# An attention and mixture-of-experts kernel: index columns named earlier in VectorE's step, weight pieces split by one line over all tiles

## The chip, the cores and the metric

One core of one Trainium2 chip runs the whole program. The metric is the device time of one execution in microseconds (us); for the kernel before, the median of three timed executions is given, and one further execution was profiled.

## What is computed

The reference is one transformer layer on 16 sequences of 56 tokens (896 tokens, width 512), all in float32:

```python
x = x + xattn(layernorm(x), ctx_4096, Wq, bq, Wk, bk)   # one head over 1500 context rows of 512 per sequence
x = x + ffn(layernorm(x), gate_w, bias, Wg, Wu, Wd, Sg, Su, Sd)

# ffn, with E = 16 experts of inner width 256, and 4 experts for each token:
scores = sigmoid(x @ gate_w.T) + bias
topk_w, topk_idx = top_k(scores, 4)
topk_w = topk_w / (sum(topk_w) + 1e-20)
z   = silu(x @ Wg[e].T) * (x @ Wu[e].T) * weight_of(token, e)
out = sum_e z @ Wd[e].T + silu(x @ Sg.T) * (x @ Su.T) @ Sd.T
```

Which tokens go to which expert is known only on the chip. With the inputs of the reference the 16 experts get 55, 484, 523, 0, 0, 470, 0, 0, 0, 6, 398, 338, 82, 102, 790 and 336 tokens (worked out from the reference alone).

## The kernel before

**Two stages.** The first stage (to about 280 us) streams the context through TensorE for eight pairs of sequences. The second stage is the feed-forward part: seven tiles of 128 tokens through the shared expert, and then the routed tiles. The change touches the second stage alone.

**Tiles and turns.** The tokens of an expert are cut into tiles of up to 128 rows. An expert with at least one token is a *turn*. The counts above give 11 turns of 1, 4, 5, 4, 1, 4, 3, 1, 1, 7 and 3 tiles, 34 tiles in all. I number these tiles u = 0 to 33; the code's own `t` is u + 7, because `SHARED` is 7 (the shared expert's tiles come first). The tables of the loop (which turn, which expert, which column of the list of rows, how many weight pieces must be asked for) are made on VectorE in `find_turns` and `fill_tables`, and go by way of TensorE (`lay_tables`) into one row of integers, `plan`. Each engine reads an entry of it into a register with `entry` (L323), which the trace shows as a `TENSOR_LOAD` on that engine's sequencer.

**Weights.** An expert's weights (1.5 MB) come by DMA into `w_raw`, one of three sets. They are split into a high and a low part, in three pieces (`THIRDS`) for each turn, 33 pieces in all: ScalarE makes `w_hi` (L896), VectorE then makes `w_lo` = `w_raw` - `w_hi` (L1279). `more_thirds(t)` on either engine makes as many pieces as the plan's entry T_PIECES for tile t asks for beyond those made; SyncE loads the set of a later turn as soon as the pieces that free it are done (the wait is on `lo_ready`). TensorE waits in `split_turn` before the first tile of a turn.

**One step of the loop.** Every engine runs its own list for tile t:

- TensorE: transpose of z(t-1) (L702), low part of the up product of t (L679 on `taken_lo`), transpose of tile t+1 (L499), down product of t-1 (L679 on `zt_hi`, then on `zt_lo`), high part of the up product of t+1 (L679 on `taken_hi`, `w_hi` and `w_lo`).
- ScalarE: `zt_hi`(t-1) (L917), `half_tanh`(t) (L912), `taken_hi`(t+1) (L907), `y_sb`(t-2) (L925, which waits until the add that last read this half of `y_sb`, that of t-4, has landed), the row numbers for the add of t-2, `add_at` (L930), and then its pieces `w_hi`.
- VectorE: `zt_lo`(t-1) (L1314), `gated_rows` and `z_rows` of t (L1335, L1323), `taken_lo`(t+1) (L1298), the routing weights `taken_w` of t+1 (`take_weight`, L1309), the row numbers for the gather of t+3, `take_at` (`name_take`, L1305), and then its pieces `w_lo`.
- GpSimd, in strict order: the gather of tile t+5 (`gather`, L444, an indirect DMA, which needs `take_at` of t+5), then the add of tile t into the output in HBM (`add`, L459, an indirect DMA that accumulates, which needs `y_sb` and `add_at` of t). The first tile of a turn also waits until every earlier add has landed, because another expert may hold the same tokens.

Of the kernel before, what the change touches and what calls it, by code (L numbers as in the profile page):

```python
# [8 lines left out]
EXPERTS, INNER, TOPK = 16, 256, 4  # L9
P = 128  # L10
# [21 lines left out]
SETS = 3  # L32
THIRDS = 3
# [4 lines left out]
SHARED = TOKENS // P  # L38
# [34 lines left out]
def moe_attention_kernel(nc, x, ctx, ctx_t, wq, bq, wk, bk, gate_t, gate_b, experts, shared,  # L73
# [14 lines left out]
    with es:  # L88
        def sb(name, shape, dt=fp32):
            return es.enter_context(nc.sbuf_tensor(name, shape, dt))  # L90
# [111 lines left out]
        upto = sb("upto", [P, 1])  # L202
# [17 lines left out]
        expert_t = sb("expert_t", [P, 1])  # L220
        col_t = sb("col_t", [P, 1])
        turn_t = sb("turn_t", [P, 1])
        size_t = sb("size_t", [P, 1])
        done_t = sb("done_t", [P, 1])
        share_t = sb("share_t", [P, THIRDS])
        ready_t = sb("ready_t", [P, THIRDS])
        thirds_t = sb("thirds_t", [P, 1])
        all_thirds = sb("all_thirds", [P, 1])
        all_turns = sb("all_turns", [P, 1])
        last_turn = sb("last_turn", [P, 1])  # L230
# [62 lines left out]
        def settle(eng):  # L293
            eng.sem_inc(waited, 1)
# [26 lines left out]
        def entry(eng, table, at, most):  # L321

            return eng.value_load(plan[0:1, bass.ds(at + table, 1)], min_val=0, max_val=most)  # L323
# [86 lines left out]
        def _(pool):  # L410
# [29 lines left out]
            def gather(t, i):  # L440

                pool.wait_ge(take_named, t - (SHARED - 1))
                settle(pool)
                nc.gpsimd.indirect_dma_start(  # L444
                    taken[i][:, :], None, h_rows[:, :], bass.IndirectOffsetOnAxis(ap=take_at[i][:, 0:1], axis=0)
                    ).then_inc(gathered[i], 16)
# [565 lines left out]
        def _(dve):  # L1012
# [237 lines left out]
            def fill_tables():  # L1250

                ch.link(nc.vector.tensor_tensor(is_turn_e[:], is_turn_e[:], iota16, ALU.mult))
                ch.mark(nc.vector.scalar_tensor_tensor(col_t[:], expert_t[:], float(TILES_MAX), upto[:], ALU.mult, ALU.add))
                ch.mark(nc.vector.tensor_tensor(size_t[:], end_t[:], first_t[:], ALU.subtract))
                ch.mark(nc.vector.tensor_tensor(done_t[:], upto[:], first_t[:], ALU.subtract))
                ch.mark(nc.vector.tensor_scalar_add(last_turn[:], all_turns[:], -1.0))
                ch.mark(nc.vector.tensor_scalar(all_thirds[:], all_turns[:], float(THIRDS), None, ALU.mult))
                ch.mark(nc.vector.tensor_tensor(is_first[:], first_t[:], upto[:], ALU.is_equal))
                ch.link(nc.vector.tensor_scalar(halves[:], half_at[:], tiles_upto[:, EXPERTS - 1:EXPERTS], None, ALU.is_lt))

                ch.mark(nc.vector.tensor_scalar(share_t[:], iota16[:, 1:1 + THIRDS], size_t[:], 1.0 / THIRDS, ALU.mult, ALU.mult))
                ch.mark(nc.vector.tensor_scalar_add(done_t[:], done_t[:], 1.25))
                ch.mark(nc.vector.tensor_tensor(tables[:, 1:2], col_t[:], first_t[:], ALU.subtract))
                ch.mark(nc.vector.tensor_scalar_min(tables[:, 2:3], expert_t[:], float(EXPERTS - 1)))
                ch.mark(nc.vector.tensor_tensor(tables[:, 4:5], turn_t[:], last_turn[:], ALU.min))
                ch.mark(nc.vector.scalar_tensor_tensor(tables[:, 5:6], first_t[:], float(SHARED), is_first[:], ALU.add, ALU.mult))
                ch.mark(nc.vector.reduce_sum(tables[:, 6:7], is_turn_e[:], axis=AX.X))
                ch.mark(nc.vector.reduce_sum(tables[:, 7:8], halves[:], axis=AX.X))
                ch.link(nc.vector.tensor_copy(tables[:, 0:1], all_turns[:]))
                ch.link(nc.vector.tensor_scalar(ready_t[:], share_t[:], done_t[:], None, ALU.is_le))  # L1270
                ch.link(nc.vector.reduce_sum(thirds_t[:], ready_t[:], axis=AX.X))
                ch.link(nc.vector.scalar_tensor_tensor(thirds_t[:], turn_t[:], float(THIRDS), thirds_t[:], ALU.mult, ALU.add))
                ch.link(nc.vector.tensor_scalar_add(thirds_t[:], thirds_t[:], float(THIRDS)))
                ch.mark(nc.vector.tensor_tensor(tables[:, 3:4], thirds_t[:], all_thirds[:], ALU.min))
                dve.wait_ge(dve_step, ch.now())
                dve.sem_inc(tables_ready, 1)

# [27 lines left out]
                nc.vector.tensor_copy(take_at[i][:], list_at[:, bass.ds(col, 1)]).then_inc(take_named, 1)  # L1305

            def take_weight(t, i):
                e = entry(dve, T_EXPERT, t - SHARED, EXPERTS - 1)
                nc.vector.tensor_copy(taken_w[:, i:i + 1], taken[i][:, bass.ds(e + DIM, 1)]).then_inc(w_ready, 1)  # L1309

# [72 lines left out]
            dve.wait_ge(hi_ready, THIRDS)  # L1383
            third_lo(2 * THIRD)
            n_inner = inner_pairs(dve)
            taken_to_lo(SHARED)
            take_weight(SHARED, 1)
            name_take(SHARED + 2, 1)

            def step(t, i):  # L1390
                z_to_lo(t - 1)
                silu_rows(t, i)
                taken_to_lo(t + 1)
                take_weight(t + 1, 1 - i)
                name_take(t + 3, 1 - i)
                more_thirds(t + 1)

            more_thirds(SHARED)
# [72 lines left out]
```

## Time and profile before

| | us |
|---|---|
| median of three executions | 553.05 |
| the three | 546.88, 553.05, 556.69 |
| the profiled execution, its own time | 548.86 |
| its span, first to last instruction | 547.1 |
| stretch of the routed loop on TensorE (first up product of tile 0 to that of tile 33) | 321.2 to 521.7 |

| engine | busy us | share of the span |
|---|---|---|
| TensorE, matmul | 490.3 | 90% |
| TensorE, weight load | 293.8 | 54% |
| VectorE | 259.4 | 47% |
| ScalarE | 155.4 | 28% |
| GpSimd | 110.8 | 20% |

### The profile page before, as it was taken

Reading aid. Unit: us, or ns where it says so; the run is one execution under the profiler, and the core shown is the slowest. Engines: PE = TensorE matmul, PEld = TensorE weight load, DVE = VectorE, ACT = ScalarE, POOL = GpSimd, SP = SyncE. Lnnn points to the kernel's source line nnn. Section 1 sums busy time; section 2 is a strip of 40 time slices with the busy share of each in tenths; the row PEclk is TensorE's granted clock in tenths of the full one; section 3 lists DMA queues with packets and bytes.
Section 4 is the critical chain, followed back from the end, with each engine's and each line's share of the span. In section 5 each row is a group of like instructions: output and inputs, shape, how many; then the busy total and the mean of one; then the engine's idle time right before and its main releaser. Section 6 shows DMA issues by size and latency. Waiting matters only on the chain.

```text
span 547.1 us, 10804 instructions
## 1 busy us (share of the span) xinstructions
PE 490.3 (90%) x2472; PEld 293.8 (54%) x2473; DVE 259.4 (47%) x707; ACT 155.4 (28%) x303; POOL 110.8 (20%) x100
## 2 busy tenths in 40 slices
PE   3999999999999999999899878989898988899970
PEld 1583535353636363543467646767676656577740
DVE  3203337373645445453448874545455646545420
ACT  0000402020203021210222263435363545444430
POOL 1000000000000000000002233444344442444431
PEclk9969999999999999999799989999898999899985
DMA  9999999999999999999646667876749585455552
GB/s 214 399 423 424 388 424 419 411 428 401 427 400 425 400 423 411 417 426 418 241 114 159 157 207 197 270 230 115 195 124 261 98 212 174 80 84 108 97 64 32
DMA packets 28231, 149.04 MB, mean 272 GB/s; under 512 B 4072, under 2 KB 4200, under 8 KB 16424
## 3 DMA queue, kind: packets, MB, share of 16 engines
q1 hardware_dynamic: 15832, 123.08, 56.6%
q0 software_dynamic: 8720, 20.21, 20.2%
q10 hardware_dynamic: 3664, 5.57, 3.3%
q8 instruction: 7, 0.11, 0.1%
q14 instruction: 8, 0.07, 0.0%
HBM read 133.84 MB, written 15.01 MB: 272 GB/s over the span
## 4 chain that ended last, share of the span: by engine, by line
PE 67%; DMA 14%; issue 6%; DVE 4%; ACT 3%; DVEq 2%; ACTq 2%; POOLq 1%; POOL 0%; SPq 0%
PE b L573 16%; PE scores L549 15%; PE b L679 14%; DMA out<-y_sb,add_at 10%; PE b L537 6%; PE b L499 4%; PE scores L679 3%; DMA w_raw<-in_experts 3%; PE scores L511 2%; PE b L563 2%; DMA w_qk<-in_wk 1%; PE b L586 1%; DVEq L323 1%; ACTq L323 1%; ACT w_hi L896 1%
## 5 line engine op out<-in xcount | busy, mean ns | idle before, releaser
L573 PE MATMUL b<-ctx_rows,probs_t 125*64 125x512 f32 (+1 forms) x384 | 86.4, 600 | 0.0
L549 PE MATMUL scores<-ctx_cols,g_t 128*64 128x500 f32 x384 | 84.8, 586 | 0.0
L459 POOL DMA_INDIRECT out<-y_sb,add_at x34 | 54.6, 1605 | 52.2 <-ACT add_at L930 21.8
L423 POOL TENSOR_TENSOR rstd<-var_eps,neg_half 128x1 f32<-128x1 f32 x16 | 8.8, 551 | 268.5 <-DVE var_eps L1021 268.5
L1279 DVE TENSOR_TENSOR w_lo<-w_raw,w_hi (+1 forms) x33 | 39.7, 1223 | 41.2 <-ACT w_hi L896 29.8
L679 PE MATMUL b<-w_hi,taken_hi 128*128 x136 | 57.5, 423 | 1.1 <-ACT taken_hi L907 1.1
L679 PE MATMUL b<-w_lo,taken_hi 128*128 x136 | 55.9, 411 | 0.0
L573 PEld LDWEIGHTS b<-ctx_rows,probs_t 125*64 125x64 f32 (+1 forms) x384 | 26.4, 138 | 48.3 <-issue 47.4
L549 PEld LDWEIGHTS scores<-ctx_cols,g_t 128*64 128x64 f32 x384 | 26.3, 137 | 48.3 <-issue 48.3
L444 POOL DMA_INDIRECT taken<-h_rows,take_at x34 | 34.1, 1002 | 76.4 <-DVE take_at L1305 74.7
L896 ACT CAST w_hi<-w_raw (+1 forms) x33 | 33.8, 1048 | 31.3 <-issue 15.1
L679 PE MATMUL b<-w_hi,taken_lo 128*128 x136 | 40.0, 416 | 0.0
L1052 DVE TENSOR_REDUCE row_max<-scores 128x1 f32<-128x1500 f32 x8 | 13.8, 1721 | 47.2 <-PE scores L549 47.2
L835 ACT COPY h_t_now<-b 128x512 f32<-128x512 f32 x7 | 4.1, 586 | 109.4 <-PE b L499 109.4
L537 PE MATMUL b<-xn_t,w_fold 128*128 128x128 f32 x256 | 33.1, 291 | 1.4 <-ACT xn_t L819 1.4
L679 PEld LDWEIGHTS b<-w_hi,taken_hi 128*128 128x128 f32 x136 | 27.3, 200 | 13.0 <-issue 7.1
L537 PEld LDWEIGHTS b<-xn_t,w_fold 128*128 128x128 f32 x256 | 31.7, 205 | 2.1 <-issue 1.1
L917 ACT CAST zt_hi<-b 128x256 fp32r<-128x256 f32 x41 | 15.2, 371 | 54.7 <-PE b L702 54.6
L1314 DVE TENSOR_TENSOR zt_lo<-b,zt_hi 128x256 fp32r<-128x256 f32 x41 | 17.2, 421 | 28.2 <-ACT zt_hi L917 26.0
L679 PEld LDWEIGHTS b<-w_lo,taken_hi 128*128 128x128 f32 x136 | 27.2, 200 | 5.6
L907 ACT CAST taken_hi<-b 128x512 fp32r<-128x512 f32 x41 | 24.1, 587 | 16.4 <-PE b L499 14.9
L1298 DVE TENSOR_TENSOR taken_lo<-b,taken_hi 128x512 fp32r<-128x512 f32 x41 | 28.1, 684 | 1.4 <-ACT taken_hi L907 1.3
(213 smaller groups left out, 682.0 us busy)
## 6 DMA issues: line engine op xcount, KB each, us to landing
ctx_rows<-in_ctx SPq DMA_DIRECT2D x48, 1024.0 KB, 15.0
ctx_cols<-in_ctx_t SPq DMA_DIRECT2D x32, 1500.0 KB, 17.8
w_raw<-in_experts SPq DMA_DIRECT2D x11, 1536.0 KB
h_rows<-h ACTq DMA_DIRECT2D x16, 115.5 KB
taken<-h_rows SPq DMA_DIRECT2D x7, 264.0 KB
out<-xs ACTq DMA_DIRECT2D x2, 784.0 KB
shared_raw<-in_shared SPq DMA_DIRECT2D x1, 1536.0 KB, 32.3
xs<-in_x ACTq DMA_DIRECT2D x12, 112.0 KB
```

Source lines behind the costliest of these rows:

```text
L444: nc.gpsimd.indirect_dma_start(taken[i][:, :], None, h_rows[:, :], bass.IndirectOffsetOnAxis(ap=take_at[i][:, 0:1], axis=0)).then_inc(gath ...
L459: nc.gpsimd.indirect_dma_start(out[:, :], bass.IndirectOffsetOnAxis(ap=add_at[i][:, 0:1], axis=0), y_sb[:, i * DIM:(i + 1) * DIM], None, c ...
L499: last = nc.tensor.transpose(bank[:, k * P:(k + 1) * P], src[:, k * P:(k + 1) * P], ident)
L537: last = nc.tensor.matmul(b7[:, m * P:(m + 1) * P], w_fold[:, k, m * P:(m + 1) * P], xn_t[:, k, :], start=(k == 0), stop=(k == KD - 1))
L549: last = nc.tensor.matmul(scores[HALF * b:HALF * (b + 1), n, 0:CHUNK], g_t[:, k, HALF * b:HALF * (b + 1)], ctx_cols[:, at:at + CHUNK], sta ...
L573: last = nc.tensor.matmul(b3[HALF * b:HALF * (b + 1), :], probs_t[0:rows_in(p), at:at + HALF], ctx_rows[0:rows_in(p), g, b, c * DIM:(c + 1 ...
L679: return nc.tensor.matmul(bank, a[:, k, :], w[:, bass.ds(at + k * n, n)], start=start, stop=stop)
L896: nc.scalar.copy(w_hi[:, bass.ds(at, THIRD)], w_raw[:, bass.ds(at, THIRD)]).then_inc(hi_ready, 1)
L907: nc.scalar.copy(taken_hi[:].rearrange("p k n -> p (k n)"), b4[:, :]).then_inc(taken_hi_ready, 1)
L1279: nc.vector.tensor_tensor(w_lo[:, bass.ds(at, THIRD)], w_raw[:, bass.ds(at, THIRD)], w_hi[:, bass.ds(at, THIRD)], ALU.subtract).then_inc(l ...
L1298: nc.vector.tensor_tensor(taken_lo[:].rearrange("p k n -> p (k n)"), b4[:, :], taken_hi[:].rearrange("p k n -> p (k n)"), ALU.subtract).th ...
L1314: nc.vector.tensor_tensor(zt_lo_cols[:], b5[:, 0:INNER], zt_hi_cols[:], ALU.subtract).then_inc(zt_lo_ready, 1)
```

## The change

It has two parts and some waits.

1. In VectorE's `step`, `take_weight(t + 1, ...)` and `name_take(t + 3, ...)` move from behind `taken_to_lo(t + 1)` to the head of the step, ahead of `z_to_lo(t - 1)`; ahead of the loop, `taken_to_lo(SHARED)` moves behind them. So within VectorE's list they stand behind the weight pieces of the step before instead of ahead of those of the same step. `take_weight` now waits for the gather of its tile to land and for `z_rows`; `gather` on GpSimd now also waits for the transposes of the tile that last held its buffer (`tt_ready`).
2. In `fill_tables`, the number of weight pieces that must have been asked for by a tile no longer follows that tile's place within its own turn, but one straight line over all tiles, (u + 1) / tiles x 3 x turns + 4. It is bounded below by what the next tile needs and above by what the three sets of weights can hold.

```diff
@@ gather
                 pool.wait_ge(take_named, t - (SHARED - 1))
                 settle(pool)
+                pool.wait_ge(tt_ready, t - 1)
+                settle(pool)
@@ fill_tables
-                ch.mark(nc.vector.tensor_tensor(size_t[:], end_t[:], first_t[:], ALU.subtract))
-                ch.mark(nc.vector.tensor_tensor(done_t[:], upto[:], first_t[:], ALU.subtract))
+                ch.mark(nc.vector.tensor_scalar(is_last[:], end_t[:], -1.0, upto[:], ALU.add, ALU.is_equal))
+                ch.mark(nc.vector.reciprocal(per_tile[:], tiles_upto[:, EXPERTS - 1:EXPERTS]))
...
+                ch.mark(nc.vector.tensor_scalar_add(line_t[:], upto[:], 1.0))
...
-                ch.mark(nc.vector.tensor_scalar(share_t[:], iota16[:, 1:1 + THIRDS], size_t[:], 1.0 / THIRDS, ALU.mult, ALU.mult))
-                ch.mark(nc.vector.tensor_scalar_add(done_t[:], done_t[:], 1.25))
+                ch.mark(nc.vector.scalar_tensor_tensor(line_t[:], line_t[:], per_tile[:], all_thirds[:], ALU.mult, ALU.mult))
+                ch.mark(nc.vector.tensor_tensor(need_t[:], turn_t[:], is_last[:], ALU.add))
+                ch.mark(nc.vector.tensor_tensor(most_t[:], turn_t[:], is_first[:], ALU.subtract))
...
-                ch.link(nc.vector.tensor_scalar(ready_t[:], share_t[:], done_t[:], None, ALU.is_le))
-                ch.link(nc.vector.reduce_sum(thirds_t[:], ready_t[:], axis=AX.X))
-                ch.link(nc.vector.scalar_tensor_tensor(thirds_t[:], turn_t[:], float(THIRDS), thirds_t[:], ALU.mult, ALU.add))
-                ch.link(nc.vector.tensor_scalar_add(thirds_t[:], thirds_t[:], float(THIRDS)))
-                ch.mark(nc.vector.tensor_tensor(tables[:, 3:4], thirds_t[:], all_thirds[:], ALU.min))
+                ch.mark(nc.vector.tensor_scalar(need_t[:], need_t[:], float(THIRDS), float(THIRDS), ALU.mult, ALU.add))
+                ch.link(nc.vector.tensor_scalar(most_t[:], most_t[:], float(THIRDS), float(SETS * THIRDS), ALU.mult, ALU.add))
+                ch.link(nc.vector.scalar_tensor_tensor(line_t[:], line_t[:], float(THIRDS + 1), most_t[:], ALU.add, ALU.min))
+                ch.link(nc.vector.tensor_tensor(line_t[:], line_t[:], need_t[:], ALU.max))
+                ch.mark(nc.vector.tensor_tensor(tables[:, 3:4], line_t[:], all_thirds[:], ALU.min))
@@ take_weight
             def take_weight(t, i):
+                dve.wait_ge(gathered[i], (t - SHARED) // 2 * 16 + 16)
+                settle(dve)
+                dve.wait_ge(z_rows_ready, t - 1)
+                settle(dve)
@@ ahead of the loop, and the step
-            taken_to_lo(SHARED)
             take_weight(SHARED, 1)
             name_take(SHARED + 2, 1)
+            taken_to_lo(SHARED)

             def step(t, i):
+                take_weight(t + 1, 1 - i)
+                name_take(t + 3, 1 - i)
                 z_to_lo(t - 1)
                 silu_rows(t, i)
                 taken_to_lo(t + 1)
-                take_weight(t + 1, 1 - i)
-                name_take(t + 3, 1 - i)
                 more_thirds(t + 1)
```

## Rows read from the trace of the kernel before

**Rows 1.** The page: engines' busy time, and TensorE's granted clock in 40 slices.
```profile
PE 490.3 (90%) x2472; PEld 293.8 (54%) x2473; DVE 259.4 (47%) x707; ACT 155.4 (28%) x303; POOL 110.8 (20%) x100
PEclk9969999999999999999799989999898999899985
```
**Rows 2.** Waits, 290 to 547 us: engine, line, releaser, total, times, longest.
```profile
POOL taken L444 <- DVE take_at L1305: 74.7, 30, 6.6
...
DVE w_lo L1279 <- ACT w_hi L896: 29.8, 15, 4.2
...
ACT y_sb L925 <- DMA out<-y_sb,add_at: 22.1, 10, 4.7
```
**Rows 3.** Waits of TensorE's matmuls from 320 us on.
```profile
PE b L679 <- ACT zt_hi L917: 7.0, 4, 2.5
PE scores L679 <- ACT zt_hi L917: 4.2, 2, 2.4
PE b L679 <- DVE zt_lo L1314: 3.0, 3, 1.5
```
**Rows 4.** Timeline of TensorE: start, us; two tiles' transposes, nothing waited for between.
```profile
481.43 0.63 PE L499 MATMUL b<-cst,taken 128*128 128x128 f32 x4
...
486.79 0.63 PE L499 MATMUL b<-cst,taken 128*128 128x128 f32 x4
```
**Rows 5.** Timeline of GpSimd around tile 4's add; idle time in brackets.
```profile
362.28 1.58 POOL L459 DMA_INDIRECT out<-y_sb,add_at  x1 [1.13 <-DMA out<-y_sb,add_at]
367.88 0.98 POOL L444 DMA_INDIRECT taken<-h_rows,take_at  x1 [4.02 <-DVE take_at L1305]
369.81 1.58 POOL L459 DMA_INDIRECT out<-y_sb,add_at  x1 [0.94 <-issue]
```
**Rows 6.** Timeline of ScalarE in the step of u = 5.
```profile
356.76 0.59 ACT L907 CAST taken_hi<-b 128x512 fp32r<-128x512 f32 x1 [0.48 <-PE b L499]
358.69 0.59 ACT L925 COPY y_sb<-b 128x512 f32<-128x512 f32 x1 [1.34 <-DMA out<-y_sb,add_at]
359.40 0.19 ACT L930 COPY add_at<-list_to 128x1 int32 x1
361.28 1.05 ACT L896 CAST w_hi<-w_raw  x1 [1.69 <-issue]
362.24 0.37 ACT L917 CAST zt_hi<-b 128x256 fp32r<-128x256 f32 x1
363.24 0.61 ACT L925 COPY y_sb<-scores 128x512 f32<-128x512 f32 x1
```
**Rows 7.** Timeline of TensorE: the late down products of u = 5, 10 and 13.
```profile
363.13 0.49 PE L679 MATMUL b<-w_hi,zt_hi 128*128 x1 [1.34 <-ACT zt_hi L917]
...
393.01 0.69 PE L679 MATMUL scores<-w_hi,zt_hi 128*128 x1 [2.39 <-ACT zt_hi L917]
...
413.63 1.19 PE L679 MATMUL b<-w_hi,zt_lo 128*128 x2 [1.53 <-DVE zt_lo L1314]
```
**Rows 8.** Granted clock in stretches of 10 us (PE, PEld, DVE, ACT, POOL; PEclk, DMA, GB/s).
```profile
390.00:400.00 10.00, 7.61 (x31) 5.99 (x32) 4.95 (x10) 4.88 (x11) 3.33 (x4) 0.83 0.40 79
...
480.00:490.00 10.00, 9.91 (x47) 7.24 (x46) 5.56 (x14) 5.10 (x11) 4.49 (x4) 1.00 0.45 87
```
**Rows 9.** Timeline of VectorE in the step of u = 3, one piece in it.
```profile
346.83 0.68 DVE L1298 TENSOR_TENSOR taken_lo<-b,taken_hi 128x512 fp32r<-128x512 f32 x1
347.50 0.15 DVE L1309 COPY taken_w<-taken 128x1 f32 x1
348.33 0.15 DVE L1305 COPY take_at<-list_at 128x1 int32 x1 [0.68 <-issue]
350.13 1.22 DVE L1279 TENSOR_TENSOR w_lo<-w_raw,w_hi  x1 [1.64 <-issue]
351.27 0.42 DVE L1314 TENSOR_TENSOR zt_lo<-b,zt_hi 128x256 fp32r<-128x256 f32 x1
```
**Rows 10.** The line of table reads: count and ns min/median/max, on VectorE.
```profile
L323 DVEq TENSOR_LOAD <-plan x99: 298/306/986, 329.0 to 522.8; - x99
```

More of the change, by code:

```diff
@@ L222, in moe_attention_kernel @@
         turn_t = sb("turn_t", [P, 1])
[L223 to L227, printed above, removed]
+        is_last = sb("is_last", [P, 1])
+        per_tile = sb("per_tile", [P, 1])
+        line_t = sb("line_t", [P, 1])
+        need_t = sb("need_t", [P, 1])
+        most_t = sb("most_t", [P, 1])
         all_thirds = sb("all_thirds", [P, 1])
```

## Prediction

> **What bounds the kernel now.** I read the page first. TensorE is busy 90% of the span, and nothing else comes near [rows 1]; the time is TensorE's work plus the gaps in it and the stretches at the lower clock. The first 280 us are not touched, so I asked the waits and the timeline only from there on.
>
> The floor of the routed loop: between two tiles' transposes lie 5.36 us with no wait [rows 4]; eight such stretches lie between 5.32 and 5.54, and I take 5.34 as the floor. Tile 0's up product starts at 321.2 and tile 33's at 521.7: 200.5 us for 33 tiles, where the floor gives 176.2. So 24.3 us of the loop are losses, and only these can move.
>
> What the losses are: TensorE waits 11.2 us for `zt_hi` in six places and 3.0 us for `zt_lo` in three [rows 3] (2.1 of the 11.2 in the last tile, behind the loop). After three of these waits the granted clock falls. The slice from 390 to 400 us has 0.83 [rows 8], which is 3.4 us at 1.2 GHz instead of 2.4, and half of that, 1.7 us, is lost; the slices from 410 and from 470 read the same. A fourth, from 320, lies at the start of the loop.
>
> Why `zt_hi` is late: in the step of u = 5 ScalarE holds back `y_sb` until 358.69, because the add that last read its buffer hasn't landed, and so `w_hi` comes at 361.28 and `zt_hi` behind it at 362.24 [rows 6]. TensorE had stood 1.34 us for it [rows 7]. ScalarE waits for an add's landing ten times, 22.1 us [rows 2]. And why does the add land late? GpSimd stands in order: the add of tile 4 starts at 369.81, though its `y_sb` began at 363.24 [rows 5, 6]. Between them stands the gather of tile 9, which waited 4.02 us for `take_at` and started at 367.88. That wait is GpSimd's largest, 74.7 us in 30 waits [rows 2]. So the chain is: `take_at` late, gather late, add late, `y_sb` late, piece late, `zt_hi` late, TensorE idle, at times a slower clock.
>
> **The change, part by part.**
>
> *A, `take_at` earlier.* `name_take` moves up nearly one tile. What holds the gather of tile 9 next is its new wait, the transposes of tile 7. These end near 361.8 (TensorE's timeline has them from 361.16, 0.63 us long). With GpSimd's usual 0.9 us from the semaphore [rows 5] the gather goes at about 362.8, 5 us sooner. The add of tile 4 then waits for `add_at`, which ends 0.7 us and a copy behind the start of `y_sb` (358.69, then 359.40 [rows 6]), and goes at about 364.9 instead of 369.8. A buffer of `y_sb` is asked for again two tiles, 10.7 us, after it was filled; an add's landing takes 5 to 8.5 us in the chain of waits, so start plus landing is now 6.7 to 10.2 us after `y_sb`. Nearly all the ten waits go; the ten turn starts, whose adds wait for the landing before, keep a remainder. Of TensorE's waits the three at u = 5, 10 and 19 hang on this alone: 1.34 and 2.39 [rows 7] and 2.48, in sum 6.2 us, with one fall of the clock (390 to 400), 1.7 us. But `zt_lo` is needed 1 us after `zt_hi`, and it comes out of VectorE: by the times below, u = 5 gets back 1.0 and u = 19 2.1 of their waits. I take 5.8 + 1.7 = **7.5 us gained**.
>
> *B, pieces on a line.* Worked out from the turns' sizes, the plan asked for pieces in 21 steps; three at once before the tiles u = 14, 22 and 23, whose turns have one tile each or follow such a one. The line asks in 23 steps: at most one a step until u = 13 and none in that step, two at once before u = 15, two before u = 22, and still three before u = 23. The burst at u = 13 cost the 1.53 us of [rows 7], 0.54 before it, and the clock's 1.7 at 410 to 420: 3.8. Against this a pair costs: `w_lo` takes 1.22 [rows 9] and `w_hi` 1.05 [rows 6], so one piece more in a step delays `zt_lo` by about 1.2, and with the copies behind it 1.5. The burst before u = 22 shrinks by one piece, but part 1 of the change puts the copies behind it: 0.3 gained. The one before u = 23 stays. Sum: 3.8 - 1.5 + 0.3 = **2.6 us gained**. SyncE's queue: the sets are freed earlier, so every load is issued no later than before, and each landed before its first piece. One exception is the third set, on which the piece of u = 1 waits now as before. The two instructions that `fill_tables` gains, at about 0.16 us, are under 0.4 us and stand beside the shared tiles; the links of the chain become one fewer. I put them at nothing.
>
 Before, this ran while VectorE would anyway have waited for ScalarE's `w_hi`: `w_lo` waited 29.8 us for it in 15 steps [rows 2]. That cover is gone in steps with a piece. From the start of `w_lo` to `zt_lo` it was 1.14 us [rows 9]; now the sequencer can run on while `w_lo` computes, and needs 0.2 + 0.4 + 1.66 + 0.2 = 2.5. So in a step where `w_hi` decides, `zt_lo` would be 1.3 later. In a step where `w_hi` is early, `w_lo` starts up to 1.66 sooner, and `zt_lo` comes no later or 0.3 sooner. With the add's wait gone `w_hi` ends 3.37 us after `taken_hi`(t+1) starts, which is about 1.95 us after the up product that follows. That puts `zt_lo` at 4.6 us behind that up product where 4.3 is wanted, and the lateness halves itself, since a late TensorE starts the next `taken_hi` late: 0.17 a step. Table reads that take 0.6 to 1.0 instead of 0.306 [rows 10] now lie behind the wait instead of under it; about one in six does, which is 0.1 a step more. So 22 steps with one piece x 0.25 = 5.5 us. The two first steps with pieces, which wait for the weights' DMA, cost 0.75 and 1.3. Sum: **7.5 us lost**. Bounds for C: nothing (if every `w_hi` is early), and 1.3 a step, 22 x 1.3 + 2 = 31 us (if none is and no slack takes it). I stand near the low end, because before the change VectorE's sequencer was as full and single-piece steps took 5.44 to 5.54 us, hardly more than the floor.
>
> A rule weighed: for a table read the row has 0.306 us at the median [rows 10]. The Trainium skill (DMA: Bandwidth & Descriptors, Latency and other measured facts) states a floor of about 0.6 us for a tensor load, which this trace contradicts in most of its 99 reads. By that figure C would be 22 x 0.6 = 13 us dearer, and the change would lose about 11.
>
> *New waits.* `take_weight` waits for the gather of t+1 with `zt_lo`, `z_rows` and `taken_lo` queued behind it, so TensorE's down product would wait for it too. That gather is now issued two tiles before; the old one went at 367.88 [rows 5] and TensorE, which never waited for a gather [rows 3], read its tile 5.9 us later. I put the wait at nothing, and at most 0.5 us at each of ten turn starts, 5 us.
>
> **Sum:** -7.5 - 2.6 + 7.5 = -2.6 us against the profiled execution's 548.86: 546.3. The tail behind tile 33 (adds that wait for each other) moves along unchanged. The three timed runs have their median at 553.05, 4.2 above the profiled one; in proportion I get 550.5. The slower runs should hold more late landings, which A removes, so I take 549.5.
>
> **The rivals.**
>
> *1, faster: the add chain was all.* If VectorE keeps up (C at nothing), the losses of rows 3 in the loop (9.1 + 3.0) and three falls of the clock (5.1) go, but for the burst before u = 23 (about 4): 13 to 14 us, 2.5%, so 539. For it: VectorE is busy 47% only [rows 1]. Against: its time is its sequencer's, which that share leaves out. Chance 0.13.
>
> *2, slower: VectorE's sequencer becomes the bound.* The place is the stretch from `w_lo` to `zt_lo`. The gains are 10.1, so it decides against the change from (10.1 - 2) / 22 = 0.37 us a step, and makes it slower by 2% from 0.87. At 0.9 a step: 20 + 2 - 10.1 = +12, 565. For it: 15 waits for `w_hi` [rows 2]; against it, the feedback above. By the Trainium skill's figure for a table read (the page and section named above) it would come out this way. Chance 0.1.
>
> *3, the gather's wait at the head of the step stalls.* +5 on top of my sum: 554.5. Chance 0.12.
>
> *4, hidden anyway.* GpSimd's adds stay late since the new wait on the transposes or the landings hold them; nothing moves but B and C: 553.05 - 2.6 + 7.5, at most 558, at least 551. Chance 0.1.
>
> **How the numbers follow.** My forecast has 0.55; with rivals 3 and 4 that gives 0.77 within 2% (about what a measurement of this kernel can tell from no change, 11 us), faster 0.13, slower 0.1. The range reaches from just above rival 1 to the far end of rival 4: 540 to 557.5. Its own spread for the forecast is 544 to 555.
>
> **What would show it.** A right: GpSimd's wait for `take_at` falls from 74.7 to under 20 us, replaced by one for the transposes; adds start 3 to 5 us sooner; `y_sb`'s wait for landings falls from 22.1 to under 6; the slice from 390 is at full clock. B right: `w_lo` comes three at a time once in the loop, and no fall of the clock stands near tile 14. C right: `w_lo` to `zt_lo` grows from 1.14 to about 2.5 us and TensorE's waits for `zt_lo` grow from 3.0 to 6 to 10 us in many small ones. I am wrong if TensorE's waits for `zt_lo` stay near 3 us (rival 1) or exceed 15 (rival 2), or if `taken_w` waits for gathers (rival 3).

## The result, and the profile after

| | before | after |
|---|---|---|
| median of 18 executions, us | 554.22 | 559.29 |
| the same, lowest to highest | 546.88 to 560.58 | 556.53 to 562.20 |
| the profiled execution, its own time | 548.86 | 556.53 |
| its span | 547.1 | 554.7 |
| routed loop on TensorE, first up product of tile 0 to that of tile 33 | 200.5 | 208.2 |

The ratio is 1.0126 (95% interval 1.0096 to 1.0156): slower by 1.3%, where I had forecast 549.5 us and at most 557.5. It leaves out executions more than 1.5% above the fastest of their kernel, seven of the kernel before and none of the changed one, and so lies above the quotient of the two medians (1.009). The profiled executions differ by 7.7 us and their loops by 7.7 us as well: all of it is in the loop.

The waits of the changed kernel from 290 us to its end (engine, line, releaser, total, times, longest), beside [rows 2, 3]:

```profile
POOL taken L446 <- DVE take_at L1309: 53.4, 17, 6.4
DVE w_lo L1283 <- ACT w_hi L898: 40.5, 25, 5.0
ACT w_hi L898 <- PE b L681: 15.6, 12, 3.4
ACT w_hi L898 <- PE scores L681: 13.5, 9, 1.8
PE scores L681 <- DVE zt_lo L1322: 12.5, 12, 2.1
ACT y_sb L927 <- DMA out<-y_sb,add_at: 7.1, 4, 4.5
PE b L681 <- DVE zt_lo L1322: 5.7, 9, 1.3
PE b L681 <- ACT zt_hi L919: 4.2, 2, 2.2
```

`y_sb` waits 7.1 us for landings where it waited 22.1: that gain came. But TensorE now waits for `zt_lo` 21 times, 18.2 us, where it was 3.4 in four (the 3.0 of [rows 3], and 0.4 for a product into `scores` that I had left out). Two rows that I had no eye for have grown: ScalarE's `w_hi` waits 29.1 us in 21 steps for TensorE's *down product* (the semaphore that `more_thirds` waits for is counted up by nothing else). In the kernel before these rows were

```profile
ACT w_hi L896 <- PE scores L679: 5.4, 4, 2.5
ACT w_hi L896 <- PE b L679: 5.1, 4, 1.6
```

Two tiles of the changed kernel, on three engines (start and duration in us, idle time in brackets). VectorE:

```profile
365.98 1.23 DVE L1283 TENSOR_TENSOR w_lo<-w_raw,w_hi  x1 [1.17 <-ACT w_hi L898]
367.44 0.15 DVE L1317 COPY taken_w<-taken 128x1 f32 x1 [0.24 <-issue]
368.27 0.15 DVE L1309 COPY take_at<-list_at 128x1 int32 x1 [0.68 <-issue]
368.42 0.42 DVE L1322 TENSOR_TENSOR zt_lo<-b,zt_hi 128x256 fp32r<-128x256 f32 x1
...
371.93 1.22 DVE L1283 TENSOR_TENSOR w_lo<-w_raw,w_hi  x1 [1.53 <-ACT w_hi L898]
373.90 0.15 DVE L1317 COPY taken_w<-taken 128x1 f32 x1 [0.74 <-issue]
375.20 0.15 DVE L1309 COPY take_at<-list_at 128x1 int32 x1 [1.15 <-issue]
375.35 0.42 DVE L1322 TENSOR_TENSOR zt_lo<-b,zt_hi 128x256 fp32r<-128x256 f32 x1
```

TensorE's last product of each down product, and ScalarE's piece behind it:

```profile
368.99 0.70 PE L681 MATMUL b<-w_hi,zt_lo 128*128 x2 [0.18 <-DVE zt_lo L1322]
...
375.92 0.70 PE L681 MATMUL scores<-w_hi,zt_lo 128*128 x2 [1.03 <-DVE zt_lo L1322]
```
```profile
364.59 1.05 ACT L898 CAST w_hi<-w_raw  x1 [0.96 <-PE scores L681]
...
370.54 1.05 ACT L898 CAST w_hi<-w_raw  x1 [0.95 <-PE b L681]
```

Read them as a ring. `zt_lo` starts at 368.42; the product on it at 368.99 (+0.57), and it ends at 369.69 (+0.70). `w_hi`, which waits for that end, starts at 370.54 (+0.85), `w_lo` at 371.93 (+1.39), and behind the two reads and copies `zt_lo` at 375.35 (+3.42). That is 6.93 us for one tile; the other half of the loop's body takes 5.61 (from 362.81 to 368.42), since there `w_lo` to `zt_lo` is 2.44. Both are over the floor of 5.34 [rows 4]. Two of the other links hardly vary: in the 21 steps in which `w_hi` waits for a down product, `w_lo` starts 1.38 to 1.39 us behind it, and in 19 of them the product starts 0.57 us behind `zt_lo`; from the product's end to `w_hi` it is 0.5 to 1.0. Before, the last link was 1.14 [rows 9]; with it the same sum gives 4.3 to 4.7 us (an estimate from the links), under the floor, so that the ring never showed.

The pair of tiles thus costs 12.5 us, where two times the floor is 10.7. In the loop TensorE's waits for `zt_lo` grew by 14.8 us, those for `zt_hi` shrank by 5.2, and the small gaps that end with "issue" or at a transpose by about 3. The three falls of the granted clock (from 321.0, 341.5 and 426.9) last 3.4, 6.8 and 3.4 us and cost as much as the four before.

### The profile page after: what moved, and what is told of

It is laid out like the page before. It is cut to its first block, busy times and chain, and to the rows that moved or that the text cites. A ratio compares the mean times of both kernels' runs of the same rounds, so it can differ in the third digit from the quotient of the medians.

```text
span 554.7 us, 10946 instructions
## 1 busy us (share of the span) xinstructions
PE 490.8 (88%) x2472; PEld 291.8 (53%) x2473; DVE 261.7 (47%) x709; ACT 156.8 (28%) x303; POOL 111.6 (20%) x100
## 4 chain that ended last, share of the span: by engine, by line
PE 60%; DMA 12%; issue 8%; DVEq 5%; ACT 4%; DVE 4%; ACTq 3%; POOLq 1%; SPq 0%; POOL 0%
PE b L575 15%; PE scores L551 15%; PE b L681 10%; DMA out<-y_sb,add_at 7%; PE b L539 6%; DMA w_raw<-in_experts 4%; DVEq L323 3%; PE b L501 3%; ACT w_hi L898 3%; PE scores L513 2%; PE scores L681 2%; PE b L565 2%; ACTq L323 2%; DMA w_qk<-in_wk 1%; DVE zt_lo L1322 1%
## 5 line engine op out<-in xcount | busy, mean ns | idle before, releaser
L446 POOL DMA_INDIRECT taken<-h_rows,take_at x34 | 34.2, 1007 | 81.7 <-DVE take_at L1309 53.4
L919 ACT CAST zt_hi<-b 128x256 fp32r<-128x256 f32 x41 | 15.2, 372 | 62.1 <-PE b L704 62.1
L501 PE MATMUL b<-cst,taken 128*128 128x128 f32 x164 | 25.0, 275 | 2.1 <-issue 1.1
```

The costliest lines, as they stand in the source:

```text
L446: nc.gpsimd.indirect_dma_start(taken[i][:, :], None, h_rows[:, :], bass.IndirectOffsetOnAxis(ap=take_at[i][:, 0:1], axis=0)).then_inc(gath ...
L501: last = nc.tensor.transpose(bank[:, k * P:(k + 1) * P], src[:, k * P:(k + 1) * P], ident)
```

## The experiments

In all tables the ratio is that of a kernel's time to that of the kernel before in the same group of runs, with its 95% interval.

### Each part alone

`plan_only` is the kernel before with the diff of `fill_tables` alone; `order_only` is the changed kernel with the old `fill_tables`.

> The kernel before with the line of pieces alone (fill_tables of the change, nothing else). Theory L (loop): the loss of the changed kernel is a closed ring: w_lo, then the two table reads and copies, then zt_lo, the down product, its yt_ready, the next w_hi, the next w_lo. With the copies in their old place that ring is 0.56 + 0.70 + 0.5 to 0.9 + 1.05 + 0.34 + 1.14 = 4.3 to 4.7 us, under the 5.34 us that TensorE needs for a tile, so the line alone costs nothing and gives what part B of the prediction had, 2.6 us, bounds 0 to 5: ratio 0.991 to 1.000. Theory P (plan): asking for a piece in step after step is what makes the tiles slow; then this kernel alone carries most of the loss, ratio 1.008 to 1.013.

> The changed kernel with the old plan of pieces: only the order on VectorE and the new waits. Theory L: the ring is 5.6 us in one of the two halves of the loop's body and 6.2 to 6.9 in the other in each step with a piece, and pieces stand in 21 steps here; about 0.85 us x 18 = 15 lost, 7 won by the earlier adds, and the bursts of three (2 more lost each with the copies behind them): ratio 1.012 to 1.022, TensorE's waits for zt_lo from 12 us up. Theory P: ratio 0.995 to 1.003.

| | ratio | interval |
|---|---|---|
| plan_only | 1.0117 | 1.0071 to 1.0164 |
| order_only | 1.0225 | 1.0176 to 1.0274 |
| both (the change) | 1.0126 | 1.0096 to 1.0156 |

The effects don't add up: the line costs 1.2% in the old order and gives back 1.0% in the new one. The waits of `plan_only` from 320 us on say a part of why it costs:

```profile
ACT y_sb L925 <- DMA out<-y_sb,add_at: 29.1, 13, 4.7
...
PE scores L679 <- ACT zt_hi L917: 8.0, 4, 3.1
PE b L679 <- ACT zt_hi L917: 7.0, 4, 3.3
PE b L499 <- DMA taken<-h_rows,take_at: 6.1, 3, 4.2
```

The line puts a piece in nearly every step, and in the old order `y_sb` is late in about every third (29.1 us in 13 waits), with the piece and `zt_hi` queued behind it: 15.0 us of waits for `zt_hi` instead of 11.2. The late add was the chain that I had read, and the line meets it more often. That explains only a part of the loss. Of the 7.8 us between the two profiled executions the loop has 3.9; the others lie ahead of it, where TensorE waits 4.2 us for the gather of tile 0. The kernel before and the changed one have no such wait, but `order_only` (3.4) and `early_read_line` (3.8) do, so that it isn't shown to come from the line.

And `order_only` has the new wait at full size:

```profile
PE b L681 <- DVE zt_lo L1320: 13.7, 13, 1.7
PE scores L681 <- DVE zt_lo L1320: 8.6, 8, 2.0
```

### Is it the gather's wait, or the number of reads behind `w_lo`?

`weight_head` has `take_weight` with its two waits at the head and `name_take` in its old place, old plan. `weight_spare1` is that and, at the head, one more read of an index column and its copy into a tile that nobody uses. `spare1` is the kernel before with only such a spare read and copy at the head:

```diff
             def step(t, i):
+                read_spare(t + 1, 1 - i, 1)    # entry(T_COL), copy of list_at into a spare column
                 z_to_lo(t - 1)
```

> The changed order and waits by half, with the old plan: take_weight with its waits for the gather and for z_rows at the head of VectorE's step, name_take where it was. Theory L: one read and copy less in the ring, 0.83 us, and less often a long table read: 4.8 us in one half of the body and 5.4 to 5.9 in the other. So 0.1 to 0.3 a step, 2 to 6 us, and nothing won on the adds: ratio 1.003 to 1.010. Theory G (the wait for the gather at the head of the step costs): the whole loss stays, and grows since the gathers are late again: ratio 1.015 or more. In its trace w_lo to zt_lo is 1.6 to 2.4 us.

> take_weight at the head as in weight_head, and behind it one more table read with a copy into a spare tile that nobody reads; name_take stays in its old place. Nothing is left out of the result. Theory L: the number of reads between w_lo and zt_lo sets the time, whatever they are for: two again, so the ring is 5.6 to 6.9 us as in order_only and the loss is back, without the earlier adds: ratio 1.018 to 1.030, w_lo to zt_lo 2.4 us and up. Theory E (the loss of order_only comes from the gathers and adds going earlier or from the wait for tt_ready): ratio as weight_head, 0.997 to 1.003.

> The kernel before with one table read and one copy of an index column into a spare tile at the head of VectorE's step, ahead of z_to_lo; everything else stays, the two old copies behind taken_to_lo too. The ring theory (zt_lo, down product, w_hi, w_lo, zt_lo) goes by what stands between w_lo and zt_lo: one read and copy of about 0.83 us makes the stretch 2.0 instead of 1.14 us and the ring 5.1 to 5.6 us, hardly over the floor of 5.34, as with take_weight alone at the head (0.9993): ratio 0.998 to 1.010, w_lo to zt_lo 1.9 to 2.3 us. The theory that VectorE's whole list is the bound (three copies now in a step of about 5.9 us, where the kernel before has two) expects 0.8 us more in each step with a piece, 22 x 0.5 or more: 1.02 or more.

| | at the head | reads in a step | ratio | interval |
|---|---|---|---|---|
| weight_head | 1 | 2 | 0.9993 | 0.9964 to 1.0022 |
| order_only | 2 | 2 | 1.0225 | 1.0176 to 1.0274 |
| weight_spare1 | 2 | 3 | 1.0371 | 1.0285 to 1.0456 |
| spare1 | 1 | 3 | 1.0156 | 1.0105 to 1.0207 |

`weight_head` has the wait for the gather and loses nothing, so that wait isn't the cause. One read behind `w_lo` is free, the second costs 2.3%: that is a threshold, as a ring that passes the floor has one. `weight_spare1` cost more than I expected (at most 1.030), and `spare1`, where I had expected at most 1.010, says why. Its VectorE, with no piece in the step:

```profile
522.46 0.42 DVE L1320 TENSOR_TENSOR zt_lo<-b,zt_hi 128x256 fp32r<-128x256 f32 x1
...
523.76 0.68 DVE L1299 TENSOR_TENSOR taken_lo<-b,taken_hi 128x512 fp32r<-128x512 f32 x1
524.56 0.15 DVE L1315 COPY taken_w<-taken 128x1 f32 x1
525.40 0.15 DVE L1306 COPY take_at<-list_at 128x1 int32 x1 [0.68 <-issue]
527.86 0.15 DVE L1311 COPY spare<-list_at 128x1 int32 x1 [2.31 <-issue]
528.01 0.42 DVE L1320 TENSOR_TENSOR zt_lo<-b,zt_hi 128x256 fp32r<-128x256 f32 x1
```

From `zt_lo` to `zt_lo` it is 5.55 us with no wait for another engine: VectorE's own list, mostly its sequencer, is over the floor of 5.34. From `w_lo` to `zt_lo` it is only about 1.5 us in the mean over the steps with one piece, so the ring isn't what holds it. I read from this that there are two bounds near the floor, the ring and the length of VectorE's list, and that a third read hits the second one. This is argued from one trace: a third read was tried only at the head, and in `spare1` TensorE also waits 4.8 us for gathers in four places, which no run separates from the list.

### The same copies elsewhere

`copies_behind` is `order_only`, and `copies_behind_line` the changed kernel, with the copies one instruction later:

```diff
             def step(t, i):
-                take_weight(t + 1, 1 - i)
-                name_take(t + 3, 1 - i)
                 z_to_lo(t - 1)
+                take_weight(t + 1, 1 - i)
+                name_take(t + 3, 1 - i)
                 silu_rows(t, i)
```

> order_only (old plan) with the two copies one place further on: behind z_to_lo(t - 1) and ahead of silu_rows(t), all waits as in the changed kernel. Theory L: no read stands in the ring (4.3 to 4.7 us again), and take_at is still named more than 2 us earlier than before, so the loss of order_only (2.2%) goes; z_rows and taken_lo come some 1.8 us later, which has slack but for a few tenths a step: ratio 0.990 to 1.006. Theory E: the same gathers, adds and waits, so ratio 1.015 to 1.023.

> The changed kernel with the two copies behind z_to_lo(t - 1): line of pieces, early adds, and no read in the ring. Theories L and Y together: both losses gone, ratio 0.980 to 0.998, best of all so far; TensorE's waits for zt_lo under 5 us and ScalarE's for landings under 8. If L is wrong it stays near the changed kernel, 1.010 and more.

| | ratio | interval |
|---|---|---|
| copies_behind | 0.9968 | 0.9930 to 1.0007 |
| copies_behind_line | 1.0009 | 0.9971 to 1.0047 |

With the same waits and the same reads, `order_only`'s ratio is lower by 2.6 points once no read stands between `w_lo` and `zt_lo`. TensorE's waits in `copies_behind` from 320 us on:

```profile
PE b L681 <- ACT zt_hi L919: 7.1, 5, 1.9
PE scores L681 <- ACT zt_hi L919: 4.3, 3, 1.5
PE b L501 <- issue: 3.8, 13, 0.5
PE b L681 <- DVE taken_lo L1300: 1.9, 6, 0.4
PE b L681 <- DVE zt_lo L1320: 1.7, 3, 0.7
```

`zt_lo` costs 1.7 us instead of 22.3. But `taken_lo` now stands behind the reads (6 waits), and the transpose behind it starts late in 13 tiles. The line's version missed its expectation (at most 0.998) by a little; `y_sb` still waited 17.5 us for landings in it, where I had expected under 8. The reads are not free there either; they are cheaper.

### The reads taken out of the stretch, the copies left in

These decide whether the reads' place is the cause. The two table entries are read in the old place, behind `taken_lo` of the step before, into two held registers; the waits and the copies stay at the head, as in the changed kernel.

```diff
+            def read_next(t):
+                dve.reg_mov(next_e, entry(dve, T_EXPERT, t + 1 - SHARED, EXPERTS - 1))
+                dve.reg_mov(next_col, entry(dve, T_COL, t + 3 - SHARED, LISTS + EXPERTS - 1))
...
             def step(t, i):
-                take_weight(t + 1, 1 - i)
-                name_take(t + 3, 1 - i)
+                take_weight(t + 1, 1 - i, dve.snap(next_e, ...))
+                name_take(t + 3, 1 - i, dve.snap(next_col, ...))
                 z_to_lo(t - 1)
                 silu_rows(t, i)
                 taken_to_lo(t + 1)
+                read_next(t + 1)
                 more_thirds(t + 1)
```

> The changed kernel with the old plan of pieces (order_only, 1.0225), but the two table entries of a step are read into held registers in their old place, behind taken_lo of the step before and ahead of more_thirds, and only the four waits and the two copies stand at the head. Same copies at the same place, so take_at is as early; only the reads (0.3 us each and what the sequencer needs to pass the register on) leave the stretch from w_lo to zt_lo. If the reads in that stretch are what costs, w_lo to zt_lo falls from 2.4 to 3.5 us to 1.3 to 1.9, TensorE's waits for zt_lo fall from 22 to under 10 us, and the ratio is 0.990 to 1.005. If the copies and the added semaphore waits cost as much as the reads, or VectorE's list of instructions as a whole is the bound wherever its parts stand, it stays at 1.015 to 1.025.

> The changed kernel itself (1.0126) with the two entries read early in the same way. If only the reads in the stretch cost, the gains that the prediction counted on now show: ratio 0.975 to 0.99, ScalarE's waits for landings about 7 us as in the changed kernel. If the list as a whole is the bound: 1.005 to 1.015.

| | reads at the head | reads behind `taken_lo` |
|---|---|---|
| old plan | 1.0225 (1.0176 to 1.0274) | **0.9895** (0.9862 to 0.9928) |
| the line | 1.0126 (1.0096 to 1.0156) | **0.9861** (0.9826 to 0.9895) |

The place of the reads alone is worth 3.3 points with the old plan and 2.6 with the line (the upper and the lower ratio were taken in different groups of runs, each against the kernel before in its own). `early_read_line` is faster than both kernels: 540.47 us in the median, where the kernel before had 549.17 beside it. Its VectorE in two tiles, which answers to the stretch of the changed kernel above:

```profile
363.27 1.23 DVE L1283 TENSOR_TENSOR w_lo<-w_raw,w_hi  x1 [2.09 <-ACT w_hi L898]
364.41 0.15 DVE L1326 COPY taken_w<-taken 128x1 f32 x1
364.48 0.15 DVE L1317 COPY take_at<-list_at 128x1 int32 x1
364.54 0.42 DVE L1331 TENSOR_TENSOR zt_lo<-b,zt_hi 128x256 fp32r<-128x256 f32 x1
...
368.41 1.23 DVE L1283 TENSOR_TENSOR w_lo<-w_raw,w_hi  x1 [1.90 <-ACT w_hi L898]
369.66 0.15 DVE L1326 COPY taken_w<-taken 128x1 f32 x1
369.80 0.15 DVE L1317 COPY take_at<-list_at 128x1 int32 x1
370.06 0.42 DVE L1331 TENSOR_TENSOR zt_lo<-b,zt_hi 128x256 fp32r<-128x256 f32 x1
```

`w_lo` to `zt_lo` is 1.27 and 1.65 us instead of 2.44 and 3.42, and these two tiles take 10.67 us (`zt_lo` from 364.54 to 375.21) instead of 12.54. The idle time has gone back in front of `w_lo`, where the reads now hide under ScalarE's work. The granted clock and busy shares of its loop (PE, PEld, DVE, ACT, POOL; PEclk, DMA, GB/s) show 86 us at full clock:

```profile
330.00:416.00 86.00, 79.34 (x356) 56.77 (x356) 45.71 (x101) 43.46 (x88) 39.27 (x30) 1.00 0.78 219
```

Its loop takes 189.9 us (323.51 to 513.41), 10.6 less than before.

### The late add, from GpSimd's side

`swap` is the kernel before with the two indirect DMAs of a step exchanged, the add of t ahead of the gather of t+5; `swap_line` adds the line. `behind_line_swap` and `early_read_line_swap` are `copies_behind_line` and `early_read_line` with the same exchange. The two `hi_first` kernels also put ScalarE's `more_thirds` ahead of `keep_y` and `name_add`:

```diff
                 taken_to_hi(t + 1)
+                more_thirds(t + 1)
                 keep_y(t - 2, i)
                 if not isinstance(t, int):
                     name_add(t - 2, i)
-                more_thirds(t + 1)
```

> The kernel before, with the two calls on GpSimd in the loop exchanged: the add of tile t, then the gather of tile t + 5 (and so at the loop's end). VectorE's order is untouched. If late adds are worth what part A of the prediction says (7.5 us and the clock), this gives all of it without the reads in the ring: adds start 3 to 5 us sooner, ScalarE's waits for landings fall from 22 to under 8 us, ratio 0.982 to 0.993. If the adds were not what held TensorE, ratio 0.997 to 1.003.

> swap (add ahead of gather on GpSimd) with the line of pieces. Theory Y: the line alone cost 1.2% because it puts a piece into nearly every step, and ScalarE makes that piece behind the y_sb that waits for an add's landing (29 us in 13 waits in plan_only), so each such wait now reaches zt_hi. With the adds early these waits are gone and the line costs nothing: ratio 0.985 to 0.998, and y_sb waits under 8 us. Theory P (pieces in step after step are slow by themselves): 1.2% above swap, 1.003 to 1.008.

> The changed kernel with its two copies between z_to_lo and silu_rows instead of at the head, and with the add ahead of the gather on GpSimd. No table read stands between w_lo and zt_lo, take_at is early, so the gather behind the add goes as soon as the add has been issued. The two theories together (ring, and late adds holding w_hi and zt_hi back) expect that both kinds of wait go: TensorE's waits for gathers under 5 us (20 in the kernel with the add first and take_at late), ScalarE's waits for landings under 10 us, ratio 0.965 to 0.985. If the landing itself (5 to 8.5 us behind the issue) sets y_sb, the order on GpSimd no longer matters once take_at is early: 0.995 to 1.003, as without the swap (1.0009).

> As the kernel before this in the list, with the add ahead of the gather on GpSimd. take_at is early, so TensorE's waits for gathers should be under 6 us (20 us in 11 where take_at was late), and the late landings of the turn starts shrink too: 0.5 per cent under the kernel before this in the list, 0.97 to 0.985. If the gathers, now 2.5 us later, are waited for by take_weight at the head of VectorE's step, it is 0.99 to 1.01.

> The kernel before with the line of pieces, the add ahead of the gather on GpSimd, and on ScalarE the pieces w_hi ahead of y_sb and add_at. If a late y_sb costs because w_hi stands behind it, the waits of ScalarE for an add's landing no longer reach w_hi and w_lo, and the ratio is 0.965 to 0.985, against 0.985 for the same kernel with y_sb first. If a late y_sb costs because zt_hi of the next step stands behind it, or if the pieces now delay y_sb, add_at and so the adds by 1.05 us, it is 0.985 to 1.005. TensorE's waits for gathers (20 us in 11 in the kernel with y_sb first) should stay.

> As the kernel before this in the list, and on ScalarE the pieces w_hi stand ahead of y_sb and add_at. If late y_sb still held w_hi back there, this gains 0.5 to 1 per cent on it: 0.96 to 0.98. If the pieces ahead of y_sb make add_at and so the adds 1.05 us later, with zt_hi of the next step behind y_sb, it loses as much: 0.98 to 1.00.

| | ratio | interval |
|---|---|---|
| swap | 0.9928 | 0.9893 to 0.9962 |
| swap_line | 0.9849 | 0.9773 to 0.9925 |
| behind_line_swap | 0.9982 | 0.9950 to 1.0014 |
| early_read_line_swap | 0.9957 | 0.9924 to 0.9990 |
| swap_line_hi_first | 1.0560 | 1.0520 to 1.0600 |
| behind_line_swap_hi_first | 1.0573 | 1.0537 to 1.0610 |

`swap` says by another way that the late add cost something, and `swap_line` points to the line costing nothing once adds are early. That is the least certain row: its executions spread from 541.8 to 556.3 us, the ratio rests on four of the ten, and the median of all ten is only 0.4% under that of before. `behind_line_swap` speaks against a large effect: `y_sb` waits 5.6 us for landings in it instead of 17.5, and TensorE 4.3 for gathers, both as I had expected, and yet it is at 0.998 and not at 0.965 to 0.985. What the exchange buys it pays for, in `swap_line`, with late gathers; TensorE from 320 us on, where the kernel before has no such wait:

```profile
PE b L500 <- DMA taken<-h_rows,take_at: 20.5, 11, 5.8
```

With early reads the exchange is a loss of 1% on `early_read_line`, where I had expected a gain of 0.5%. The other case that I had put down came instead: every gather now stands behind a whole add and its waits, and `take_weight` at the head of VectorE's step waits for it, 15.2 us in 8 steps, and TensorE with it:

```profile
DVE taken_w L1327 <- DMA taken<-h_rows,take_at: 15.2, 8, 5.1
PE b L502 <- DMA taken<-h_rows,take_at: 13.0, 9, 3.0
```

`hi_first` was my worst expectation. I had priced the piece ahead of `y_sb` at its 1.05 us. TensorE's waits in `swap_line_hi_first`:

```profile
PE b L500 <- DMA taken<-h_rows,take_at: 40.3, 20, 5.1
```

Its ScalarE shows where that comes from:

```profile
377.09 0.59 ACT L908 CAST taken_hi<-b 128x512 fp32r<-128x512 f32 x1 [1.85 <-PE b L500]
379.59 1.05 ACT L897 CAST w_hi<-w_raw  x1 [1.91 <-PE scores L680]
380.54 0.58 ACT L926 COPY y_sb<-b 128x512 f32<-128x512 f32 x1
```

`w_hi` waits 1.91 us for the down product of t-1, and `y_sb` of t-2, which needs no such thing, now stands behind it; the add follows `y_sb`, and the gather the add. GpSimd's adds wait 77.9 us for `add_at` in 19 places, where it is 28.6 in 11 in `swap_line`, and the granted clock from 320 us to the loop's end is 0.91 in the mean instead of 0.98. It is the same wait for the down product that closes the ring, and I had missed it a second time. This chain is read from the trace; no run takes it apart.

## Why the prediction was wrong, point by point

**The failed step is C's feedback.** It said that `w_hi` ends 3.37 us after `taken_hi`(t+1) starts, and that "the lateness halves itself, since a late TensorE starts the next `taken_hi` late". `taken_hi` isn't what `w_hi` waits for. `more_thirds` on ScalarE waits for `yt_ready`, the down product of the tile before, and that product waits for `zt_lo`. So a late `zt_lo` makes the next `w_hi` late by the whole amount, and nothing is halved; in 21 steps `w_hi` waited for that product. The ring's length replaces the floor as the time of a tile. The right question was not how much later `zt_lo` comes, but whether the ring (0.57 + 0.70 + 0.5 to 0.85 + 1.39 + the stretch from `w_lo`) passes 5.34. With the 2.5 that I had worked out for the stretch it does: 5.66 to 6.0. All of these but the 2.5 stood in the trace of before.

**Its size.** I took 7.5 us for C in all. `early_read_line` is 7.6 us under the kernel before, the changed kernel 7.0 over it, each beside the kernel before in its own group of runs, and between the two stand only the reads. Their place costs 14.6 us, twice the term. That is 0.63 us for each of the 23 steps that ask for pieces (of these 20 ask for one, not the 22 of my sum). A and B together gave those 7.6 us where I had 10.1; so 7.1 of the 9.6 us that the sum is off are C. The mechanism is that of rival 2, which decides against the change from 0.37 a step and makes it slower by 2% from 0.87; it had 0.1. Its stated ground, that VectorE's sequencer time is left out of its 47% [rows 1], was right, its counterargument was the feedback. My sign for it, more than 15 us of waits for `zt_lo`, came: 18.2.

**The argument that VectorE's sequencer "was as full" before** and lost little was wrong: then the reads lay in a stretch where VectorE waited for `w_hi` anyway. The list of instructions kept its length, the ring didn't.

**The slow half of the body.** I added 0.1 us a step for long table reads. In the half that carries the loop's branch, `w_lo` to `zt_lo` is 2.93 to 2.95 us where both reads take their usual 0.3, and in the other half 2.44: the branch is worth 0.5, which I had not counted. The rest of the 3.42 above is a long read, 0.774 us, ahead of `take_at` at 375.20. I had not looked at the two halves apart.

**A was right in the main, and nearly in size.** The slice from 390 is at full clock, as said (1.00 in the windows view, 0.83 in [rows 8]), and waits for landings fall from 22.1 to 7.1 us (I had said under 6). The add of tile 4 starts 2.8 us behind its `y_sb` (371.48 against 368.67) instead of 6.6: 3.8 sooner. With the ring out of the way A is worth 1.05% or 5.8 us (`early_read`, with its copies and waits at the head), against the 7.5 gained that I had forecast. Of the three waits for `zt_hi` that A named, the 1.34 at u = 5 and the 2.39 at u = 10, with the clock's fall behind it, are gone in `early_read`. The third, at u = 19, stays: 2.54 us where it was 2.48, behind a `y_sb` that still waits 3.33 for a landing. All of TensorE's waits for `zt_hi` still sum to 11.3 us there, since others came at the loop's start (1.21 and 2.27). GpSimd's wait for `take_at` fell only to 53.4 in the changed kernel, not under 20, as the head of VectorE's step itself had become late.

**B was treated as independent, and is not.** -2.6 us was forecast. It is +1.2% in the old order, -1.0% in the changed one (though that is a difference of two groups of runs) and -0.3%, within the error, once the reads are early. `w_lo` comes in threes once in the loop, as said. The term that failed is the pair of pieces before tile 15, which I had put at 1.5 us: in `early_read_line` that tile takes 9.9 us (408.9 to 418.8), 4.6 over the floor, with a wait of 3.4 for `zt_hi` and a fall of the clock, where in `early_read` tile 14, with its three pieces, takes 8.0, also with a fall. The changed kernel has its fall at 426.9 in the same tile 15, where I had said that none would stand near tile 14.

**No cost of the new waits shows**: `taken_w` has no wait for a gather in the changed kernel, and `weight_head` is at 0.9993. Rival 3 is out there (its mechanism came in `early_read_line_swap`, with the gathers behind the adds), rival 1 too (18.2 us of waits for `zt_lo`), and rival 4 (waits for landings did fall).

**The rule weighed.** The Trainium skill (DMA: Bandwidth & Descriptors, Latency and other measured facts) puts a tensor load at about 0.6 us at least. The trace of before has 0.306 at the median [rows 10], that of `early_read_line` 0.305 in 106 reads, and the trace decides. That by this figure the change would have lost about 11 us, near the 7 measured, is a coincidence: the dear part was that the reads stood in a ring, not that each was long.

**What stays open.** Taking away ScalarE's wait for the down product, the most direct cut of the ring, wasn't tried, nor `name_take` alone at the head: in both, buffers would have been overwritten while they are still read. The ring is therefore shown by the stretch from `w_lo` to `zt_lo` (lengthened, shortened, reads moved out) and by its other links in the trace, not by a run without that wait. Whether the length of VectorE's list is a bound by itself, why the line alone costs 1.2% in the old order, and why `behind_line_swap` gains so little stay open. Why `plan_only`'s and the changed kernel's clock falls come where they do is only read off their gaps.

## What to carry to other kernels

Before an instruction is moved on one engine, close the loop: follow what it delays, through every engine, back to itself one tile later, and compare that ring's length with the time of a tile on the engine that bounds. A ring just below the floor is invisible in the waits and costs its whole excess in every tile once something is put into it. When an operand must come earlier, move the copy that publishes it and leave the sequencer's part (the table read) where the engine waits anyway.

## What the runs showed of the hardware that I had not expected

- A table read with its copy takes 0.83 us of VectorE's time [rows 9] of which the copy is 0.15; with the entry held in a register, two such copies start 0.07 and 0.14 us apart (364.41 and 364.48, 369.66 and 369.80), at the end of `w_lo`.
- A table read on VectorE mostly takes 0.3 us, at times up to 0.986 [rows 10]; the branch of the loop adds about 0.5 us to VectorE's stretch of the half that carries it (2.95 against 2.44).
- In `spare1`, with three reads instead of two, VectorE's list takes 5.55 us in a step without a piece, while VectorE is busy 48% of the span.
- An earlier indirect add in GpSimd's strict order is paid for with a later gather: 20.5 us of waits of TensorE in 11 places in `swap_line`, where there were none.
